# Edge messages of a graph network: 21 of 32 output columns on VectorE, 11 on GpSimd, and the bias part as a 33rd column

## What is computed

```python
eh = relu(e_feat @ en1_w.T + en1_b)                   # [E, 128]
w_e = (eh @ en2_w.T + en2_b).reshape(-1, D, D)        # a 32 x 32 matrix per edge
for _ in range(STEPS):                                # 6 steps
    msg = einsum('ei,eio->eo', out[src], w_e)
    agg = segment_sum(msg, dst) + conv_bias
    out = h = gru_cell(relu(agg), h, ...)
```

## Time and profile before

| | us |
|---|---|
| median of 3 runs (lowest, highest) | 38341.23 (38295.71, 38341.59) |
| time of the profiled execution | 38293.46 |
| its span | 38291.7 |
| DVE busy over the span | 27081.4 (71%) |
| POOL busy | 29657.2 (77%) |
| PE busy | 27942.1 (73%) |
| ACT busy | 11786.0 (31%) |

### The profile page before, as it was taken

How to read it: one execution, slowest core, us unless ns; L and a number is a source line. 1 busy time by engine, 2 the same in 40 slices (tenths; PEclk the granted TensorE clock), 3 DMA queues, 4 the chain that set the end, 5 groups by cost and what they waited for, 6 DMA issues and landing times. The chain is left out here.

```text
span 38291.7 us, 454886 instructions
## 1 busy us (share of the span) xinstructions
PE 27942.1 (73%) x97246; PEld 17043.7 (45%) x97247; DVE 27081.4 (71%) x45800; ACT 11786.0 (31%) x26941; POOL 29657.2 (77%) x30158
## 2 busy tenths in 40 slices
PE   5333346655653333899989998999899989999998
PEld 5333334455653333444444444444444444444444
DVE  7443432222531111899989999999999899989998
ACT  0000011111200000344444444444444444444444
POOL 1776777677247677799879988998899789979997
PEclk8555556655655555999999999999999999999999
DMA  0220012311311011111111111111111111111111
GB/s 19 47 48 26 23 51 82 69 28 28 89 26 14 14 14 14 43 46 47 42 45 45 46 41 46 46 47 39 47 46 47 39 47 47 47 40 46 47 47 39
DMA packets 1452380, 1590.44 MB, mean 42 GB/s; under 512 B 953756, under 2 KB 1115535, under 8 KB 1346959
## 3 DMA queue, kind: packets, MB, share of 16 engines
q1 hardware_dynamic: 743720, 1056.16, 8.7%
q0 software_dynamic: 645120, 473.02, 7.6%
q10 hardware_dynamic: 63360, 59.50, 0.5%
HBM read 1342.34 MB, written 246.33 MB: 41 GB/s over the span
## 5 line engine op out<-in xcount | busy, mean ns | idle before, releaser
L1999 PE MATMUL l3m_p_w<-en,l3m_hid 128*128 128x512 f32 x39936 | 19494.9, 615 | 1244.1 <-DVE l3m_prod L2079 1134.0
L2057 DVE TENSOR_REDUCE l3m_xg<-l3m_prod 128x32 f32<-128x1024 f32 x9984 | 12022.8, 1204 | 0.0
L1918 POOL DMA_INDIRECT l3m_xg<-wide_table,l3m_mt x9984 | 9776.2, 979 | 2639.5 <-issue 1506.2
L1927 POOL TENSOR_TENSOR l3m_prod<-l3m_rest,l3m_xg 128x384 f32<-128x384 f32 x9984 | 10093.2, 1011 | 282.4 <-ACT l3m_rest L1973 105.3
L1999 PEld LDWEIGHTS l3m_p_w<-en,l3m_hid 128*128 128x128 f32 x39936 | 6834.4, 191 | 6393.3 <-issue 4867.2
L1973 ACT COPY l3m_rest<-l3m_p_w 128x384 f32<-128x384 f32 x9984 | 4772.1, 478 | 11362.0 <-PE l3m_p_w L1999 11358.1
L2075 DVE TENSOR_TENSOR l3m_prod<-l3m_p_w,l3m_xg 128x512 f32<-128x512 f32 x9984 | 6752.9, 676 | 153.6 <-DMA l3m_xg<-wide_table,l3m_mt 134.1
L2015 PEld LDWEIGHTS l3m_p_sum<-room,l3m_apart 128*125 128x125 f32 x21120 | 3942.5, 197 | 5633.5 <-issue 5633.5
L1961 ACT ACTIVATE l3m_apart<-iota_lo,l3m_lo 128x125 f32<-128x125 f32 x10560 | 4195.1, 401 | 0.0
L2015 PE MATMUL l3m_p_sum<-room,l3m_apart 128*125 x21120 | 3332.5, 246 | 687.2 <-issue 607.0
L872 POOL DMA_INDIRECT l2a_rows<-table,l2a_mt x1664 | 1586.7, 954 | 1637.0 <-DMA l2a_mt<-dst_meta 1130.1
(11 more groups left out here) (368 smaller groups left out, 21007.8 us busy)
## 6 DMA issues: line engine op xcount, KB each, us to landing
l3m_hid<-hid_t SPq DMA_DIRECT2D x624, 1024.0 KB, 5.2
l3m_xg<-wide_table,l3m_mt POOLq DMA_INDIRECT x9984
hid_t<-l_hid SPq DMA_DIRECT2D x110, 1024.0 KB, 4.0
order_src_bk<-dst_bucket SPq DMA_DIRECT2D x52, 808.0 KB
order_dst_bk<-src_bucket SPq DMA_DIRECT2D x52, 808.0 KB
l_rec<-by_dst SPq DMA_DIRECT2D x110, 272.0 KB
l_xg<-table,l_mt POOLq DMA_INDIRECT x1760
l1a_xg<-table,l1a_mt POOLq DMA_INDIRECT x1760, 2.4
```

The source lines that it names most:

```text
L1918: pool.indirect_dma_start(xg[s][:, j, 0:2 * D], None, wide_table[:, :], bass.IndirectOffsetOnAxis(ap=mt[s][:, j, 0:1].bitcast(I32), axis=0 ...
L1927: pool.tensor_tensor(o_i(prod[j % RING][:, OWN:HD]), o_i(rest[j % RING][:, :]), state_of(s, j, REST), ALU.mult).then_inc(pooled, 1)
L1999: ins = pe.matmul(p_w[j % 2][:, c * 512:(c + 1) * 512], hid[s][:, j * P:(j + 1) * P], en2[:, c * 512:(c + 1) * 512], start=True, stop=True)
L2057: dve.tensor_reduce(xg[s][:, j, 2 * D:3 * D], o_i(prod[j % RING][:, :]), AX, ALU.add).then_inc(msgs, 1)
```

## The change

There are four parts.

1. **Message stage.** VectorE takes 21 outputs (512 and 160 columns) and GpSimd 11 (352 columns). Each `prod` buffer becomes 32 rows of 33 elements; ScalarE writes the gathered bias part of an output into its 33rd element (`bias`), so the reduction over 33 elements yields the finished message. `join` leaves VectorE; in its place ScalarE copies four tiles' messages to the ring (`keep`). GpSimd waits for `copied` only; ScalarE's copy waits for `pooled` and `msgs` of tile t-4. `LATER` goes from 6 to 8, `add` from tile 8 to 10, `clear` from 11 to 13.
2. **Order.** TensorE forms positions piece by piece as counts come, with a banded matrix of ones and 8 products of 512 columns that add up in PSUM; VectorE then picks each row's 32 of 512 (one multiplication, one reduction).
3. **`l1a`.** The squares added in a turn are those of the group before.
4. `PLACE` goes from 97 to 91, and VectorE's table `step_d` goes, since ScalarE now reads the place in the ring.

```diff
-                OWN = 20 * D
-                REST = HD - OWN
+                OWN = 21
+                REST = HD - OWN * D
...
-                prod = [ph.sb(f"prod{r}", [P, HD]) for r in range(RING)]
+                prod = [ph.sb(f"prod{r}", [P, D, D + 1]) for r in range(RING)]
...
-                LATE, LATER = 2, 6
+                LATE, LATER = 2, 8
...
                             pool.wait_ge(copied, t + 1)
-
-                            pool.wait_ge(msgs, t + 1)
-                            pool.tensor_tensor(o_i(prod[j % RING][:, OWN:HD]), o_i(rest[j % RING][:, :]),
-                                               state_of(s, j, REST), ALU.mult).then_inc(pooled, 1)
+                            pool.tensor_tensor(prod[j % RING][:, OWN:D, 0:D], o_i(rest[j % RING][:, :]),
+                                               state_of(s, j, D - OWN), ALU.mult).then_inc(pooled, 1)
...
                             act.wait_ge(pooled, t + 1)
-                            act.copy(rest[j % RING][:, :], p_w[j % 2][:, OWN:HD]).then_inc(copied, 1)
+                            act.sem_inc(begun, 1)
+                            act.wait_ge(msgs, t + 1)
+                            act.copy(rest[j % RING][:, :], p_w[j % 2][:, OWN * D:HD]).then_inc(copied, 1)
...
+                        def bias(i, s, j):
+                            t = (i * 2 + s) * G + j
+                            if j == 0:
+                                act.wait_ge(rows_in[s], i * (16 * G) + 16 * G)
+                            act.copy(prod[j % RING][:, :, D:D + 1], xg[s][:, j, D:2 * D, None]).then_inc(biased, 1)
+
+                        def keep(g, s, q):
+                            n = G // PARTS
+                            act.wait_ge(msgs, g * G + ((q + 1) * n + MSGS))
+                            at = act.snap(ring_regs[s], min_val=0, max_val=(RB - 1) * G)
+                            act.copy(msg[:, bass.ds(at + q * n, n), :],
+                                     xg[s][:, q * n:(q + 1) * n, 2 * D:3 * D]).then_inc(joined, 1)
...
+                                copy(i, s, j)
+                                bias(i, s, j)
+                                distance(i, s, j)
+                                if j == 0 and not first:
+                                    keep(g - 1, 1 - s, 2)
+                                elif j == 4 and not first:
+                                    keep(g - 1, 1 - s, 3)
+                                elif j == 8:
+                                    keep(g, s, 0)
+                                elif j == 12:
+                                    keep(g, s, 1)
+                                elif j == 13:
+                                    clear(g, s)
...
-                            dve.tensor_reduce(xg[s][:, j, 2 * D:3 * D], o_i(prod[j % RING][:, :]), AX,
+                            dve.wait_ge(biased, t + 1)
+                            dve.tensor_reduce(xg[s][:, j, 2 * D:3 * D], prod[j % RING][:, :, :], AX,
                                               ALU.add).then_inc(msgs, 1)
-
-                        def join(g, s, q):
...
                                 dve.wait_ge(ranked, c + 1)
-                                dve.tensor_scalar(pos[:, :], p_pos[:, 0:CC], -1.0, None, ALU.add)
+                                dve.tensor_tensor(own[:, :, :], p_pos[:, :].rearrange("p (a t) -> p a t", t=CC),
+                                                  turn16[:, :, None].broadcast_to([P, SPAN, CC]), ALU.mult)
+                                dve.drain()
+                                dve.tensor_reduce(rank[:, :], own[:, :, :].rearrange("p a t -> p t a"), AX, ALU.add)
+                                dve.drain()
+                                dve.tensor_scalar(pos[:, :], rank[:, :], -1.0, None, ALU.add)
...
-                            pe.wait_ge(placed, c + 1)
-                            for t in range(CC):
-                                ins = pe.matmul(p_pos[:, t:t + 1], by_col[:, t, :], ones[0:K, 0:1],
-                                                start=True, stop=True)
+                            for n in range(PIECES):
+                                pe.wait_ge(placed, c * PIECES + (n + 1))
+                                ins = pe.matmul(p_pos[:, :], band[0:K, (PIECES - 1 - n) * SPAN:(PIECES - 1 - n) * SPAN + P],
+                                                count[0:K, n * PIECE:(n + 1) * PIECE], start=n == 0, stop=n == PIECES - 1)
```

More of the change, by code:

```diff
@@ L51 @@
 EPS = 1e-5
-PLACE = 97
+PLACE = 91
 W = NB * D
@@ L121, in build @@
         before = sb("before", [P, P])
+        band = sb("band", [P, 2 * P - P // 8])
+        turn16 = sb("turn16", [P, P // 8])
         same_f = sb("same_f", [P, P])
@@ L1855, in build @@
                 rows_in = [ph.sem(f"rows_in{s}") for s in range(2)]
-                distances, hits, mats, used, copied, pooled, msgs, joined, summed, added, cleared, begun = (ph.sem(n) for n in (
-                    "distances", "hits", "mats", "used", "copied", "pooled", "msgs", "joined", "summed", "added",
-                    "cleared", "begun"))
-                LATE, LATER = 2, 6
+                distances, hits, mats, used, copied, pooled, msgs, joined, biased, summed, added, cleared, begun = (ph.sem(n) for n in (
+                    "distances", "hits", "mats", "used", "copied", "pooled", "msgs", "joined", "biased",
+                    "summed", "added", "cleared", "begun"))
+                LATE, LATER = 2, 8
                 EARLY = 4
@@ L1977, in clear @@
                             act.copy(p_sum[s][0:LO, :], none[:, :]).then_inc(cleared, 1)
-                        with act.Fori(0, TG // 2) as i:
-                            for s in range(2):
-                                for j in range(G):
-                                    copy(i, s, j)
-                                    distance(i, s, j)
-                                    if j == 11:
-                                        clear(i * 2 + s, s)
+                        def bias(i, s, j):
[3 more added lines that the diff above has]
+                            act.copy(prod[j % RING][:, :, D:D + 1], xg[s][:, j, D:2 * D, None]).then_inc(biased, 1)
@@ new lines, in keep, with group @@
+                        def keep(g, s, q):
[4 more added lines that the diff above has]
+                                     xg[s][:, q * n:(q + 1) * n, 2 * D:3 * D]).then_inc(joined, 1)
+                        def group(i, s, first=False):
+                            g = i * 2 + s
+                            act.load([ring_regs[s]], block_at[0:1, bass.ds(g, 1)])
+                            for j in range(G):
+                                copy(i, s, j)
[11 more added lines that the diff above has]
+                                    clear(g, s)
@@ L1986, in _ @@
+                        act.sem_inc(joined, JOINED)
+                        group(0, 0, first=True)
+                        group(0, 1)
+                        with act.Fori(1, TG // 2) as i:
+                            group(i, 0)
+                            group(i, 1)
+                        keep(TG - 1, 1, 2)
+                        keep(TG - 1, 1, 3)
                         with act.Fori(TG // 2, PG // 2) as i:
```

59 lines of the change are left out of this document (27 added, 32 removed).

## The result

The changed kernel takes 37,648.42 us (median of four runs, 37,569.83 to 37,657.25), the kernel before, run beside it, 38,341.41 (38,295.71 to 38,346.58). The ratio is 0.9815, with a 95% interval of 0.9803 to 0.9828. The forecast was 37,590.

A forecast was written before the change was run, and what follows sets the result against it. GpSimd was taken to set the pace at 2.168 us a tile. From 38,293.5, -699 (product), +6 (step ends) and -21 (orders) gave 37,579.5; 10 for the median made 37,590 us, range 37,400 to 37,950.

The forecast's parts named there:

- GpSimd alone sets the time of a tile: Message stage: GpSimd paces and its product shrinks in proportion; 37,440 to 37,640 us, chance 0.68.
- I take 0.070, between the two rows: GpSimd's product, 384 to 352 elements: 0.070 us less a tile, between IOTA and MEMSET bounds; -699 us in all.
- 1.92 + 0.066 = 1.99: VectorE's tile with 32 more columns in second product and reduction; 2.02 us with the add, below GpSimd's 2.098.
- the sign that I had named: VectorE in message stage: idle time ahead of the reductions, ended by GpSimd, some 0.07 us a tile.
- 1.31: ScalarE's us per tile with the added copies, of a 2.098 period: hidden unless something in its fixed order blocks.
- C: Ring: half the gain lost to late copies, 37,930 us, chance 0.10; sign: ScalarE-ended idle time ahead of GpSimd's products.
- +6 in all: End of each message step: last two `keep`s and two more TensorE sums, some 1 us each; 0 to 20 in all.
- as predicted: The two orders: first-chunk wait for positions falls from 14.06 us, -10.6 each, -21 us together (-25 to 0).
- B: VectorE becomes the bound at 2.02 us a tile if GpSimd gains more than forecast; 36,850 us, chance 0.06.
- D: No change: the saving of 32 elements is lost in writing rows of 33; 38,270 us, chance 0.05.
- E: Slower: GpSimd's product writes 11 separate rows, priced at 20 ns a row; 39,790 us, chance 0.11.
- GpSimd's pace shows no trace of the joins: Argument against VectorE becoming the bound: GpSimd's products take 1.01 us with or without a join, its gap stays 0.16.

The follow-up runs named there:

- own20_new: The changed kernel with the old split, 20 outputs for VectorE and 12 for GpSimd: 38,227.95 us, ratio to before 0.9984.
- own22_new: The changed kernel with 22 outputs for VectorE and 10 for GpSimd: 37,274.6 us, ratio to before 0.9735.
- own21_alone: The kernel before with only the split changed, 21 outputs for VectorE and 11 for GpSimd, joins still on VectorE: 37,689.7 us, ratio 0.9843.
- the added SBUF operation: The changed kernel with 22 VectorE outputs plus an unused VectorE addition, both inputs in SBUF, every fourth tile: 38,285.75 us, one run.
- spare_psum: The changed kernel with 22 VectorE outputs plus an unused VectorE addition, one input in PSUM, every fourth tile: 37,748.33 us, one run.
- own23_new: The changed kernel with 23 outputs for VectorE and 9 for GpSimd: 37,583.19 us, one run.
- own_mixed: The changed kernel with 21 VectorE outputs in tiles 1, 4, 7, 10 and 13 of a group, 22 in the others: 37,182.31 us, ratio 0.9710.

## Why the prediction was right

*The pace.* That GpSimd alone sets the time of a tile held exactly: the period followed its product, 2.168 to 2.102, and own20_new gave it back (2.172).

*The size.* The step "I take 0.070, between the two rows" was a little high: the product shrank by 0.066, just under the lower bound of 0.067 from the MEMSET, which makes 658 us instead of 699. From 384 to 288 elements it loses 0.208, thus 2.17 ns an element with a fixed part of 0.18 us, between the IOTA's 0.127 and the MEMSET's 0.204 as assumed; the three steps of 32 elements lose 0.066, 0.068 and 0.074, and the first is the smallest. The Trainium skill's addition of 2,048 elements (GPSIMD Engine Reference, "Elementwise — side-by-side cycle accounting") had given an estimate of 0.067; the trace agrees within 0.001.

*VectorE.* "1.92 + 0.066 = 1.99" is what it takes where it catches up. It was to show idle time ended by GpSimd ahead of the reductions, some 0.07 us a tile. It waits there, but the wait is in the distance of starts, with 0.3 us of idle time ended by GpSimd in 3,000: the sign that I had named was the wrong one. Its floor is the 2.070 of own22_new less 0.03 for 32 elements, 2.04, where the forecast had 2.02; the wait for TensorE once in a group makes half of that difference.

*ScalarE* is busy 1881.52 of 3,500 us (15,500 to 19,000), 1.13 a tile instead of 1.31: its records overlap, and a copy of 32 elements, 0.25 us by itself, delays the next start by less. Over the whole run it now waits for buffers that GpSimd frees (the row below). Nothing is lost by it. GpSimd does wait for ScalarE, 101.9 us in all, and such a wait was named as the sign of C; but all 96 of these waits lie in the last 16 tiles of a step, where GpSimd has no gather left to issue, and the kernel before had 105.3 us of them in the same place. Where gathers run there is none.

```profile
ACT l3m_rest L1985 <- POOL l3m_prod L1937: 4171.5, 4193, 1.3
```

*The end of each step.* "+6 in all" was -28: 21 between the steps, 7 in their last tiles. `keep` adds 0.4 us behind the last reduction, yet the last sum ends 0.6 earlier, and the first gather of the next step comes 4.2 us earlier (165.0 us behind the last product, where it was 169.2). What was left out of the sum is the start: `joined` was raised by VectorE behind a memset of 3 us, and GpSimd's first gather waited for it, 1.1 us behind its end; ScalarE raises it at once, the gather starts while the memset still runs, and the wait is for the list of rows. The lists of POOL's waits, before and after:

```profile
POOL l3m_xg L1918 <- DVEq L2097: 1034.3, 6, 188.1
```
```profile
POOL l3m_xg L1930 <- DMA l3m_mt<-dst_meta: 847.7, 5, 185.6
```

*Order.* GpSimd's idle time is 594.3 and 585.3 us instead of 604.6 and 596.0 (the first fence below; the second is the changed kernel): -21.0, as predicted. The two orders together end only 18 us earlier, since their DMAs take 2.7 more. VectorE's wait for TensorE is 109.3/52 = 2.1 us, where about 2 were named.

```profile
L518 POOL DMA_INDIRECT by_src<-order_dst_rec,order_dst_idx x1664 | 1625.9, 977 | 596.0 <-issue 507.0
```
```profile
L531 POOL DMA_INDIRECT by_dst<-order_src_rec,order_src_idx x1664 | 1630.2, 980 | 594.3 <-issue 504.6
L531 POOL DMA_INDIRECT by_src<-order_dst_rec,order_dst_idx x1664 | 1628.1, 978 | 585.3 <-issue 507.1
```

*The rest.* The sum was 37,579.5 for the profiled execution, which took 37,569.8. That this is within 10 us is luck, since terms cancel: 41 too much for the product, 34 too little for the steps' ends, and 17 too little ahead of the steps (38 instead of 21; `l1b` alone is 23 shorter, and `l1a` takes 6 back). That the forecast lies 58 below the median comes from the median's distance to the profiled execution, 79 where I had set 10.

*The rivals.* B's premise, that more gain would run into VectorE, was right and only a split away: own22_new stands on it, at 2.070, where the forecast's figures give 2.02 + 0.033 = 2.05. C and D did not occur. E's price was too high by a factor of 80. "GpSimd's pace shows no trace of the joins" was true of the kernel before, where all joins but twelve were held and none ran into a gather. The twelve, in the last tiles of the steps, start together with a product and take 0.28; it is the product that takes 1.14 to 1.21 there instead of 1.01. GpSimd can be held too, then, and own21_alone shows the same with gathers, 0.08 us each time. The Trainium skill's rule of mutual exclusion (SBUF — State Buffer, "Who interferes with whom") agrees in that wherever a join or the added SBUF operation meets a product of GpSimd in these runs, one of the two takes longer, and spare_psum agrees with its limit to two SBUF inputs.

## What to carry to other kernels

When one engine sets the pace, what a change takes off it comes back tile for tile, and what it takes off the others comes back only once the split has moved on to them: try the next size up as soon as the edits that clear the second engine are in, and mix sizes where the two bounds lie on both sides. A "busy" engine that is held by another shows it in the mean of one instruction form (0.912 us for work of 0.27), and such an operation changes its price with the phase of the two engines, so price it at both ends. At the start of a stage, look also at which engine raises the first semaphore, and what stands ahead of it there.

## What the runs showed that I had not expected

- A VectorE addition with both inputs in SBUF that starts up to 0.66 us *ahead* of GpSimd's product, while a gather still runs, is held over that whole product (up to 1.68 us for 0.27 of work), and one that starts just ahead of a gather makes it 0.08 us longer (1.06 instead of 0.98).
- The same loss turned a kernel that gained 1.6% at 21 outputs into one that lost 0.9% at 22.
- From 16,000 to 18,800 us TensorE is busy 2,713.6 to 2,716.4 of 2,800 us, at a granted clock of 1.00, in the changed kernel, own22_new, own23_new and own_mixed alike, though their periods are 2.102, 2.070, 2.099 and 2.061: its busy share says nothing here of what bounds them.
